# Where layer 1's causal mask meets the row maxima: a second product on PE, or an operand of VectorE's instruction

## What is computed

```python
scores = jnp.einsum('bnqd,bnkd->bnqk', q, k) * scale
causal = jnp.triu(jnp.ones((S, S), dtype=bool), k=1)
scores = jnp.where(causal, -jnp.inf, scores)
attn = jax.nn.softmax(scores, axis=-1)
```

## Time and profile before

| | |
|---|---|
| runs | 907.22, 907.61, 911.10 us |
| median | 907.61 us |
| the profiled execution | 910.58 us, its span 908.5 us |
| granted TensorE clock over the span | 0.936 |
| PE busy | 798.4 us (88%), 3907 instructions |
| DVE busy | 490.1 us (54%), 1369 instructions |
| ACT busy | 367.3 us (40%) |

### The profile page before, as it was taken

One profiled execution on the slowest core, in us unless ns is written; L12 is line 12 of the kernel. 1 busy time (PEld: TensorE's weight loads), 2 busy tenths in 40 slices (PEclk: granted clock), 3 DMA queues, 4 the chain that ended last, 5 costly groups with the idle time before them and its releaser, 6 DMA issues. The chain is left out here.

```text
span 908.5 us, 11697 instructions
## 1 busy us (share of the span) xinstructions
PE 798.4 (88%) x3907; PEld 419.0 (46%) x3908; DVE 490.1 (54%) x1369; ACT 367.3 (40%) x581; POOL 98.5 (11%) x111
## 2 busy tenths in 40 slices
PE   5599999999998899999987778878998889979886
PEld 3222435344345456666653333434464445533665
DVE  2743852763645522222265794888665955664363
ACT  3388785875842011111142205534423532146130
POOL 0000000000000111111811101221011101012000
PEclk9699999999999999999978798978999979889999
DMA  6558025024061061111117580007200450000000
GB/s 203 152 189 277 10 85 160 1 82 117 24 205 50 18 183 42 45 46 46 29 49 220 148 234 4 1 25 210 68 1 2 129 173 1 2 1 24 12 12 24
DMA packets 51582, 75.02 MB, mean 83 GB/s; under 512 B 7606, under 2 KB 44762, under 8 KB 49226
## 3 DMA queue, kind: packets, MB, share of 16 engines
q1 hardware_dynamic: 49660, 69.26, 25.3%
q0 software_dynamic: 1872, 5.11, 2.2%
HBM read 46.57 MB, written 27.66 MB: 82 GB/s over the span
## 5 line engine op out<-in xcount | busy, mean ns | idle before, releaser
L616 PE MATMUL ps<-arena 128*128 128x256 f32 (+5 forms) x1084 | 340.8, 464 | 22.4 <-DVE arena L1203 5.0
L616 PEld LDWEIGHTS ps<-arena 128*128 128x128 f32 (+1 forms) x1084 | 206.7, 201 | 118.5 <-issue 75.6
L921 ACT ACTIVATE arena<-ps 128x1024 f32<-128x1024 f32 x128 | 124.2, 1027 | 32.8 <-PE ps L650 32.6
L1016 ACT ACTIVATE arena<-ps 128x1024 f32<-128x1024 f32 (+3 forms) x128 | 83.2, 705 | 94.2 <-PE ps L854 93.9
L1369 DVE TENSOR_REDUCE arena<-ps 128x1 f32<-128x512 f32 (+3 forms) x176 | 101.1, 635 | 35.8 <-PE ps L832 31.8
L721 PE MATMUL ps<-arena 128*128 x184 | 88.0, 602 | 1.2 <-DVE arena L1274 1.2
L830 PE MATMUL ps<-arena 96*128 96x128 bf16 (+3 forms) x256 | 66.4, 316 | 14.6 <-DVE arena L1369 9.4
L608 PE MATMUL ps<-arena 128*128 128x128 f32 (+3 forms) x237 | 42.0, 320 | 41.2 <-DVE arena L1086 17.1
L650 PE MATMUL ps<-arena 96*128 96x512 bf16 x256 | 71.5, 391 | 6.7 <-DMA arena<-q_stacks_dram 3.6
L1456 POOL TENSOR_SCALAR_AFFINE_SELECT arena<-arena 128x512 f32<-128x512 f32 x64 | 43.1, 675 | 286.4 <-ACT arena L1016 286.1
L664 PE MATMUL ps<-arena 128*32 128x512 f32 x512 | 69.7, 612 | 2.9 <-DVE arena L1148 2.7
(11 more groups left out here) (144 smaller groups left out, 723.7 us busy)
## 6 DMA issues: line engine op xcount, KB each, us to landing
arena<-stacks_dram SPq DMA_DIRECT2D x16, 768.0 KB, 6.3
arena<-in_gate_up_proj SPq DMA_DIRECT2D x8, 1024.0 KB, 9.5
arena<-q_stacks_dram SPq DMA_DIRECT2D x8, 768.0 KB, 5.9
stacks_dram<-arena SPq DMA_DIRECT2D x16, 384.0 KB, 3.3
arena<-in_down_proj SPq DMA_DIRECT2D x8, 512.0 KB, 8.7
stacks_dram<-arena SPq DMA_DIRECT2D x16, 256.0 KB, 3.6
q_stacks_dram<-arena SPq DMA_DIRECT2D x8, 384.0 KB, 4.1
yg_dram<-arena SPq DMA_DIRECT2D x23, 128.0 KB, 1.7
```

What stands on the lines that cost most here:

```text
L616: last = nc.tensor.matmul(dst[0:rows, lo:hi], a, w, start=(n == 0), stop=(n == len(pairs) - 1))
L921: nc.scalar.activation(probs[:, 2 * p:2 * p + 2, :], ps[:, 2 * p:2 * p + 2, :], ACT.Exp)\
L1016: nc.scalar.activation(cprobs[:, i % 2, 2 * p:2 * p + 2, P * kt:S], ps[:, 2 * p:2 * p + 2, P * kt:S], ACT.Exp).then_inc(exp_done[p], 1)
```

## The change

The mask becomes a full row of 512 columns, `cmask`: 384 zeros, then the upper triangle times -1e30. For each head the slice of its last w columns is added to the w scores. PE's 256 mask products are gone; PE frees its part of the step after the score products alone. DVE runs one `tensor_tensor_reduce` for each head (256 in place of 176 reduces), which reads the scores in PSUM and the mask in SBUF, writes the sum back over the scores in PSUM, and puts the row's maximum in `mmax`. Of a step's heads only the last frees the bank. The maxima are no longer negated there; step cM waits for the counted instructions (`settle`) and negates in its two instructions. At the start of the kernel one memset more is run.

```diff
--- before.py
+++ after.py
@@ -179,7 +179,7 @@
         identb = place([P], BF16)
         upper = place([P])
         ones = place([P])
-        negmask = place([P], BF16)
+        cmask = place([S], BF16)
         cosb = place([NT, HD])
         sinb = place([NT, HD])
         iotae = place([E])
@@ -318,7 +318,7 @@
         c_a_t = place([NC_, S])
         c_x3_t = place([NC_, S])
         y2 = place([NT, C])
-        mneg = place([NT, NH])
+        mmax = place([NT, NH])
         mparts = place([NT, 2, NH], BF16)
         m_t = place([S], BF16)
         cattn = place([S])
@@ -827,10 +827,8 @@
                     dst = take(pe, step)
                     w = P * (qt + 1)
                     for g in range(nh):
-                        nc.tensor.matmul(dst[:, w * g:w * (g + 1)], cq_stack[0:STACK, b % 2, h0 + g, cols(qt)],
-                                         ck_stack[0:STACK, b % 2, h0 + g, 0:w], start=True, stop=True)
-                        last = nc.tensor.matmul(dst[:, w * g + P * qt:w * (g + 1)], identb, negmask,
-                                                start=False, stop=True, skip_group_check=True)
+                        last = nc.tensor.matmul(dst[:, w * g:w * (g + 1)], cq_stack[0:STACK, b % 2, h0 + g, cols(qt)],
+                                                ck_stack[0:STACK, b % 2, h0 + g, 0:w], start=True, stop=True)
                     last.then_inc(full_of(step), 1)
                 elif n == "cM":
                     pe.wait_ge(m_parts, b + 1)
@@ -1108,7 +1106,8 @@
             v.wait_ge(s_const, 48)
 
             tick(nc.vector.tensor_copy(identb, ident))
-            link(nc.vector.tensor_scalar(negmask, upper, NEG, None, ALU.mult))
+            tick(nc.vector.memset(cmask[:, 0:S - P], 0.0))
+            link(nc.vector.tensor_scalar(cmask[:, S - P:S], upper, NEG, None, ALU.mult))
             for step in a_steps:
                 n, b, i = step
                 if n == "rw":
@@ -1366,15 +1365,22 @@
                     w = P * (qt + 1)
                     if i == 0 and b:
                         v.wait_ge(m_parts, b)
-                    nc.vector.tensor_reduce(mneg[:, qt, h0:h0 + nh],
-                                            filled(v, step)[:, 0:nh * w].rearrange("p (h n) -> p h n", n=w),
-                                            AX.X, ALU.max, negate=True).then_inc(free_of(step), 1)
+                    src = filled(v, step)
+                    for g in range(nh):
+                        last = nc.vector.tensor_tensor_reduce(
+                            out=src[:, w * g:w * (g + 1)], in0=src[:, w * g:w * (g + 1)], in1=cmask[:, S - w:S], scale=1.0,
+                            scalar=-3e38, op0=ALU.add, op1=ALU.max, accum_out=mmax[:, qt, h0 + g:h0 + g + 1])
+                        if g < nh - 1:
+                            tick(last)
+                    last.then_inc(free_of(step), 1)
                 elif n == "cM":
 
                     for i in range(len(MAXES) - UNITS, len(MAXES)):
                         consumed(v, ("max", b, i))
-                    link(nc.vector.tensor_copy(mparts[:, :, 0, :], mneg))
-                    nc.vector.tensor_tensor(mparts[:, :, 1, :], mneg, mparts[:, :, 0, :], ALU.subtract).then_inc(m_parts, 1)
+                    settle()
+                    link(nc.vector.tensor_scalar(mparts[:, :, 0, :], mmax, -1.0, None, ALU.mult))
+                    nc.vector.scalar_tensor_tensor(out=mparts[:, :, 1, :], in0=mmax, scalar=-1.0, in1=mparts[:, :, 0, :],
+                                                   op0=ALU.mult, op1=ALU.subtract).then_inc(m_parts, 1)
                 elif n == "cF":
                     v.wait_ge(o_evac, HG * (B + b) + i + 1)
                     rows_of(co_sb, i, c_a_t, cattn, rden, cat_ready, 2 * b)
```

## The result

The changed kernel took 921.19 us (median of 4 executions, 916.60 to 926.20) beside 908.41 us for the kernel before (4 executions): a ratio of 1.0138, 95% interval 1.0073 to 1.0202. Two later measurements of the same pair gave 1.0183 (1.0149 to 1.0217) and 1.0141 (1.0103 to 1.0179). It is slower by 1.4 to 1.8%. Its 16 executions spread from 915.65 to 928.21 us, more than the 69 of the kernel before in the same four groups of runs (904.47 to 913.13), and the shorter ones had the higher granted clock: 918.45 us at 0.929, 928.21 us at 0.917.

What follows compares the result with a forecast made beforehand. DVE was taken to lead in batch 0, both engines near their limit in batch 1, PE in batches 2 and 3. Terms 6.7 + 2.3 + 2.8 + 1 = +12.8 us on the 907.61 median gave 920.4, predicted as 920.5; range 907 to 940.

Steps and rivals of the forecast that it cites:

- d: DVE's extra time for each new instruction to put out its maximum; 0.10 us taken, 64 a batch, bounds 0 to 0.28.
- PE's saving: Mask products gone from PE: worth 0 in batch 0, 0.9 us in batch 1, 2.0 each in batches 2 and 3.
- the clock: PE idles longer inside bursts, and half-clock stretches double its work's time: between 0 and 4 us, 1 taken.
- Main part at a reduce's rate per column: DVE's new instruction costs what a reduce costs per column: a batch's 20480 columns stay at 21.3 us.
- ACT's row: Profile row of ACT's squares with accumulator output: two records, the read holding the next instruction back by 0.09 us.
- Batch 0, +6.7: DVE-bound from about 515 us: of 7.7 us added DVE work, 1 us falls in slack and 6.7 land.
- the DVE term: A batch's added DVE work: 1.3 us for 20 more instructions plus d for each of 64; batch 0 hides 1 us.
- Batch 1, +2.3: Waits for PE hide the first six steps' 2.2 us; later steps add 3.2, PE saves 0.9: net +2.3 us.
- Batches 2 and 3, +2.8: Each: four-head steps delay projections, 2.0 us; closing burst +1.4; PE's products -2.0; net +1.4 each.
- The rival of a free accumulator: Accumulator goes out at no cost, PE's saving decides: 903 us. Chance of d below 0.05: 0.20, of faster: 0.07.
- that of no overlap: DVE's accumulator read does not overlap: 939 us at d = 0.20, 953 at 0.28; chance 0.16 for d above 0.15.
- The half rate in PSUM: DVE reading and writing the same bank runs at half rate: 21.3 us more a batch, 988 us; chance 0.04.

## Why the prediction was right, and where it was right by luck

The forecast was 920.5 us, and 920.9 to 925.2 were measured. The sign and the main mechanism held: DVE's added work delays the maxima where DVE leads. The sizes of the terms did not hold, and they made up for each other. That is luck, and not a little of it. The prediction says itself that with d between 0.01 and 0.05 the result is within 0.5%, and d came out at 0.05. With it the prediction's terms, as reckoned for the two halves of the batches (-1 to +1, and +3.6 to +5.6), give with the 1 us of clock 911 to 915 us. The missing 6 us or more are about what two terms lacked that were wrong the other way: PE's saving (5 us forecast, 1.7 measured with DVE unchanged) and the clock (1 us forecast, 4.5 measured on the projections). The two are not separate: with the products gone and DVE unchanged, the projections take 4.0 us more.

- **Main part at a reduce's rate per column**: held. The write into the scores' bank adds no time per column.
- **d = 0.10 by ACT's row**: about twice too large. DVE's read costs 0.05, as the second part of its own search stands 0.05 behind the first: the nearest row was on the same engine, and I passed it by for one whose name fitted better. The Trainium skill's two instructions (VectorE: DVE Perf Modes, Two Vector instructions with no wait between them) are what the trace shows, 256 records of each kind. DVE's added work was 18.5 us, not 30.8, and its busy time rose by 17 us, not by the 30 that were to show it.
- **Batch 0, +6.7**: +6.2 in the profiled execution, 3.7 and 3.9 in the two profiles whose third projection missed the half clock (43.6 and 43.9 us, against 40.0). Without the projections the stage is 28.7 us long before and 31.8 to 32.2 in all seven profiles that run the new instruction on every head of batch 0: DVE's part is 3.1 to 3.5 us, against the 3.6 that the DVE term gives with d = 0.05. What varies is the projections: 11.3 us before, 14.0 to 14.5 in five, 11.7 and 12.0 in two.
- **Batch 1, +2.3**: +0.7. With PE's products put back it is +1.9, so DVE's price there is 1.9 us, not 3.2, and PE's saving 1.2, where I had 0.9.
- **Batches 2 and 3, +2.8 with steps of four heads as the cause**: the direction held, the cause is not settled. With the instruction only in steps of one head their cost was all but gone, in one profile. And the size, +1.4 each for a measured +4.6 and +1.1 in one execution and +2.2 and +2.8 in another, came out of d = 0.10, which was wrong, and of a saving of PE that I set at 2.0 a batch.
- **PE's saving, 5 us in all**: the term that failed. Without any change on DVE it is worth 1.7 us (0.1 to 3.5), and beside the new instruction nothing that can be measured in the total (1.2 us in batch 1). In batch 0 the runs show how: I had put its saving at nothing, and in the profile without the products it was a loss of 3.2 us, all of it projections at half clock. For the later batches this was not followed product by product.
- **The clock, +1**: too small by some 3 to 4 us. The projections of the four stages took 4.5 us more in the profiled execution, 3.0 of them in batch 0. My reason, that idle stretches are DVE's already, overlooked that a stretch at half clock reaches into the fp32 projections, where PE is busy all the time, and makes them up to 1.9 times as long (3.75 for 1.96 us). What half clock costs PE's other work was not taken apart.

The rival of a free accumulator would have needed d below 0.02 to 0.03, that of no overlap one above 0.2; neither held. The half rate in PSUM did not occur.

Open is why the same stage runs at 0.76 in five profiles and at 0.81 in two (43.6 and 43.9 against 46.1 to 46.3 us). The five have their first projection at 3.75 us and their third at 3.35 to 3.65, the two at 2.8 to 3.0 and 1.95, so the half-clock stretches lie elsewhere in the stage; what places them was not found. The first does not decide the third: with one plain reduce for each head and PE's products they are 3.75 and 1.95. A product more for each head did not decide it: both levels occur with it and without. Open too is what the executions of 920 to 928 us spend more than the profiled ones.

## What to carry to other kernels

Count the distance from start to start in a burst, on both engines, before moving work between them: here 0.06 us a product on PE against 0.05 us for each accumulator read and 0.065 us for each extra instruction on DVE. The PE side looked like 227 ns each in the table of groups. A reduce over several heads at once should be kept: splitting it into one for each head cost 4.9 us here (2.9 to 6.9). And work taken off PE in a stretch where it waits anyway may leave the fp32 work behind it at a lower clock, as in batch 0 here (0.88 to 0.74): look at the granted clock by stage, not only at the sum, and take the length of a stage apart into the work that the clock stretches and the rest. The rest was the steadier number, 31.8 to 32.2 us in seven profiles whose stage lengths differ by 2.7 us.

## What the runs showed of the hardware

- DVE's reduction with an accumulator output is recorded as a main part and a read of 135 to 143 ns; the read and the next main part start together, and a pair costs 0.05 us more than a plain reduce at 128, 256, 384 and 512 columns (0.25, 0.38, 0.52 and 0.65 us from start to start against 0.20, 0.33, 0.47 and 0.60).
- DVE reading and writing the same PSUM bank ran at (0.65 - 0.25) / 384 = 1.04 ns a column, as a read alone, (0.60 - 0.20) / 384.
- Within one kernel the executions' time went with the granted clock (918.45 us at 0.929, 928.21 us at 0.917), and the changed kernel spreads wider (915.65 to 928.21) than the kernel before (904.47 to 913.13). Why it does was not tested.
